# One core, three fused stages: turnings moved ahead, scores on array quarters, and weights split in small parts

## The reference

```python
hid = silu(xm @ W_h + b_h)                      # xm: patch of 16 samples and 16 ones
h = hid @ W_o + b_o + xm @ W_r + b_r
h = h + identity_attention(layernorm(h))        # corr = centred @ centred.T, softmax, @ x
y = layernorm(h)
for l in range(2):
    q, k, v = split(shift_token(y) @ wqkv[l])
    q, k = rotary(l2norm(q) * q_scale, l2norm(k) * k_scale)
    y = y + local_attention(q, k, v) @ wo[l]    # causal inside a window of 128 tokens
    a, g = split((layernorm(shift_token(y)) * lg + lb) @ w1 + b1)
    y = y + (a * gelu(g)) @ w2 + b2
out = h + y
```

## Time and profile before

| | us |
|---|---|
| median of 3 runs | 2766.34 (2763.4 to 2767.32) |
| the profiled execution | 2766.27 |
| its span, first to last instruction | 2764.5 |
| TensorE busy | 2641.3, 96% |
| DVE busy | 1918.9, 69% |
| ACT busy | 1719.4, 62% |
| POOL busy | 1399.9, 51% |
| mean granted TensorE clock | 0.984 of full speed |

### The profile page before, as it was taken

One profiled execution on the slowest core, in us unless ns is written; L12 is line 12 of the kernel. 1 busy time (PEld: TensorE's weight loads), 2 busy tenths in 40 slices (PEclk: granted clock), 3 DMA queues, 4 the chain that ended last, 5 costly groups with the idle time before them and its releaser, 6 DMA issues.

```text
span 2764.5 us, 67543 instructions
## 1 busy us (share of the span) xinstructions
PE 2641.3 (96%) x23040; PEld 2257.0 (82%) x23040; DVE 1918.9 (69%) x3771; ACT 1719.4 (62%) x4181; POOL 1399.9 (51%) x1466
## 2 busy tenths in 40 slices
PE   6999999858999999997999998999999999999998
PEld 4888888747888888886888886788888887788887
DVE  5777777547777777776655555777777777666664
ACT  3666666536777778775444444778777777444442
POOL 7888888658666666663100005866666666000000
PEclk9999999979999999999999999999999999999999
DMA  1111111111111111112211111111111111122221
GB/s 31 32 38 35 36 35 35 53 56 48 40 40 39 37 38 40 39 34 77 65 56 50 57 48 39 49 37 40 40 37 37 40 40 52 60 80 79 79 72 46
DMA packets 165603, 130.23 MB, mean 47 GB/s; under 512 B 23239, under 2 KB 163689, under 8 KB 165462
## 3 DMA queue, kind: packets, MB, share of 16 engines
q1 hardware_dynamic: 163157, 119.80, 14.0%
q0 software_dynamic: 2304, 8.47, 1.0%
HBM read 77.47 MB, written 50.33 MB: 46 GB/s over the span
## 4 chain that ended last, share of the span: by engine, by line
PE 70%; POOL 2%; SPq 2%; DVE 2%; issue 1%; DMA 1%; ACT 0%; POOLq 0%; DVEq 0%
PE const_banks L1291 6%; PE const_banks L1292 6%; PE const_banks L1293 6%; PE const_banks L1302 6%; PE const_banks L1304 6%; PE const_banks L1303 6%; PE const_banks L1389 5%; PE const_banks L1371 4%; PE const_banks L1399 4%; PE const_banks L1357 4%; PE const_banks L1418 3%; PE const_banks L1419 3%; PE const_banks L1420 3%; PE const_banks L1346 2%; PE const_banks L1344 2%; PE const_banks L1345 2%
## 5 line engine op out<-in xcount | busy, mean ns | idle before, releaser
L1019 ACT ACTIVATE attn_E<-const_banks,attn_nbias,attn_rn 128x128 f32<-128x128 f32 x1024 | 454.9, 485 | 8.6 <-DVE attn_nbias L1185 8.5
L958 POOL TENSOR_TENSOR attn_rn<-attn_ssm,const_neg_half 128x8 f32<-128x8 f32 x128 | 211.1, 1650 | 413.8 <-DVE attn_ssm L1201 313.6
L939 POOL TENSOR_TENSOR ffn_rstd<-ffn_var,const_neg_half 128x4 f32<-128x4 f32 x32 | 32.3, 1010 | 678.5 <-DVE ffn_var L1118 678.5
L952 POOL TENSOR_TENSOR attn_qk<-attn_rot_a,attn_rot_b 128x1024 f32<-128x1024 f32 x128 | 305.8, 2389 | 66.2 <-issue 55.6
L1180 DVE TENSOR_REDUCE attn_neg_top<-const_banks 128x8 f32<-128x1024 f32 x128 | 156.8, 1225 | 233.9 <-PE const_banks L1389 233.9
L1302 PE MATMUL const_banks<-weights_w_hi,attn_xT_hi 128*128 128x512 f32 x768 | 315.9, 411 | 2.6 <-ACT attn_sq L1059 2.4
L1304 PE MATMUL const_banks<-weights_w_hi,attn_xT_lo 128*128 128x512 f32 x768 | 304.6, 397 | 0.0
L1303 PE MATMUL const_banks<-weights_w_lo,attn_xT_hi 128*128 128x512 f32 x768 | 303.4, 395 | 0.0
L1217 DVE SCALAR_TENSOR_TENSOR ffn_gated<-const_banks,weights_b_col,ffn_gate 128x512 f32<-128x512 f32 (+1 forms) x192 | 143.7, 748 | 215.0 <-ACT ffn_gate L1086 207.8
L1291 PE MATMUL const_banks<-ffn_xT_hi,ffn_w_hi 128*128 128x512 f32 x704 | 282.4, 401 | 6.9 <-DVE ffn_xT_lo L1130 5.4
L1293 PE MATMUL const_banks<-ffn_xT_hi,ffn_w_lo 128*128 128x512 f32 x704 | 279.3, 397 | 0.0
(11 more groups left out here) (171 smaller groups left out, 7929.6 us busy)
## 6 DMA issues: line engine op xcount, KB each, us to landing
attn_x_res<-xa SPq DMA_DIRECT2D x128, 128.0 KB, 4.7
xb<-attn_x_new SPq DMA_DIRECT2D x128, 128.0 KB, 1.7
ffn_x_<-xb SPq DMA_DIRECT2D x32, 512.0 KB
h<-ident_h SPq DMA_DIRECT2D x64, 128.0 KB, 1.7
xa<-ident_n SPq DMA_DIRECT2D x64, 128.0 KB, 1.7
attn_x_<-xa SPq DMA_DIRECT2D x128, 64.0 KB
xa<-ffn_x_new SPq DMA_DIRECT2D x16, 512.0 KB, 3.4
ffn_add<-h SPq DMA_DIRECT2D x16, 512.0 KB, 6.9
```

The costliest lines, as they stand in the source:

```text
L952: pool.tensor_tensor(qk[:, slot].rearrange("p a n -> p (a n)"), rot_a[:].rearrange("p a h d -> p (a h d)"), rot_b[:].rearrange("p a h d -> ...
L958: pool.tensor_tensor(rn[:, slot, HEADS:], ssm[:, HEADS:], c["neg_half"][:, HEADS:], ALU.pow).then_inc(s["rn_done"], 1)
L1019: last = act.activation(E[:, r, i], ps_s[:, r, i * P:(i + 1) * P], ACT.Exp, bias=nbias[:, r, i:i + 1], scale=rn[:, slot, h:h + 1], accum_o ...
```

## The change

In the first stage: TURN stands behind SCORE in the step and no longer behind WEIGH, so that WEIGH of one step, SCORE and TURN of the next, and CENT follow each other; DONE and STORE come one step earlier; `idle` is gone; layer 0's attention weights are loaded in the steps 12, 27 and 42 and split in parts of 128 columns, one a step; POOL's list is written out. In the layers' attention: q and k, and then E, are turned before the weighting; the scores use the quarters of the array, and leave out the masked one; on ACT the high half of the output comes last; on DVE the division of E stands between the two rotary products, and the sums of squares stand ahead of the maximum; two one-element activations (`ask`) call for the tables of Exp and Gelu ahead of their first use.

```diff
-    OUT, STAT, CENT, SCORE, WEIGH, TURN, DONE, STORE = 8, 9, 10, 11, 12, 13, 14, 15
+    OUT, STAT, CENT, SCORE, WEIGH, TURN, DONE, STORE = 8, 9, 10, 11, 12, 13, 13, 14
...
-                    pool.tensor_tensor(idle[:], zero[:], zero[:], ALU.add)
                     pool.tensor_copy(hid_hi[:, slot, k], hid[:, half]).then_inc(hi_done, 1)
...
-                    if isinstance(t, int) and t in (ROWS + 5, ROWS + 7, ROWS + 9):
-                        piece = (t - ROWS - 5) // 2
-                        weights.load_attention(pool, 0, piece)
-                        weights.split_attention(pool, 0, piece)
-                run_eights(pool, ROWS, STORE, body)
+                    weights.attention_part(pool, t)
+                run_eights(pool, ROWS, STORE, body, loop=False)
...
+    def attention_part(self, pool, t):
+        for piece, first, parts in ((0, 14, 12), (1, 29, 12), (KD, 44, KI * D // P)):
+            if t == first - 2:
+                need(pool, self.a_low, self.parts)
+                self.load_attention(pool, 0, piece)
+            if first <= t < first + parts:
+                if t == first:
+                    pool.wait_ge(self.loaded, 16 * self.loads)
...
+                cols = slice((t - first) * P, (t - first + 1) * P)
+                pool.tensor_copy(hi[:, cols], self.stage[:, cols]).then_inc(self.a_high, 1)
+                self.parts += 1
+                pool.wait_ge(self.a_high, self.parts)
+                pool.tensor_tensor(lo[:, cols], self.stage[:, cols], hi[:, cols].bitcast(F32), ALU.subtract
+                                   ).then_inc(self.a_low, 1)
...
# ACT, attention of a layer
+                if step == 0 and layer:
+                    act.activation(ask[:], c["neg_half"][:, 0:1], ACT.Exp)
...
+                if step == ROWS + 4:
+                    act.activation(ask[:], c["neg_half"][:, 0:1], ACT.Gelu)
...
# TensorE, attention of a layer: the block of lag 3, which stood last, now follows the output products
+                if on(3):
+                    b = t - 3
+                    need(pe, s["et_done"], 2 * b)
+                    for r, dst in ((0, ps_q), (1, ps_k)):
+                        need(pe, s["kT_done" if r else "qT_done"], min_int(b + 2, L + ROWS))
+                        need(pe, s["en_done"], 2 * b + r + 1)
+                        for j in range(HEADS // 2):
+                            last = pe.transpose(dst[:, j * P:(j + 1) * P], E[:, r, j], c["ident"][:])
+                        last.then_inc(s["e_ps"], 1)
...
-                    need(pe, s["qT_done"], b + 1)
-                    need(pe, s["kT_done"], b + 1)
                     for j in range(HEADS // 2):
                         for r in range(2):
                             part = slice(r * HD, (r + 1) * HD)
-                            last = pe.matmul(ps_s[:, r, j * P:(j + 1) * P], qT[part, j], kT[part, j], start=False,
-                                             stop=True, skip_group_check=True)
+                            pe.matmul(ps_s[0:HD, r, j * P:j * P + HD], qT[part, j, 0:HD], kT[part, j, 0:HD],
+                                      start=False, stop=True, skip_group_check=True)
+                            last = pe.matmul(ps_s[HD:P, r, j * P:(j + 1) * P], qT[part, j, HD:P], kT[part, j],
+                                             start=False, stop=True, skip_group_check=True)
                     last.then_inc(s["s_ps"], 1)
```

96 lines of the change are left out of this document (50 added, 46 removed).

## The result

The changed kernel takes 2724.5 us (median; 2724.05 to 2724.97 in 4 runs) against 2764.9 for the kernel before (2763.0 to 2767.3 in 4 runs): a ratio of 0.9853, 95% interval 0.9836 to 0.9871. It is faster by 40 us; 52 were forecast, and 2724.5 lies in the range. Whether the 40 us came from the terms of the sum is another matter. The profiled execution of the changed kernel has a span of 2723.2 us.

The account below looks back on a forecast made before the run. The tensor engine was taken to bind, so its list had to get shorter. Attention 25, first stage 11, drain 12 and small terms 4 sum to 52 us off 2766.3: 2714 us, range 2700 to 2728.

Parts of the forecast that it names:

- The scores: Attention: scores in the rule's quarters save 0.12 + 0.10 us a row, 0.21 taken; no gain from the masked quarter.
- Does anything else then bind?: Attention: the loop through DVE takes 9.91 us, 0.08 under the tensor engine's 9.99, so it was taken as hidden.
- rival 1: Attention: the DVE loop binds, or the scores' change is still paid; about 10.2 us a row, 2739 us; chance 0.25.
- Rivals 3 and 4: Scores: quarters sharing rows run serially (3: about 2769 us, chance 0.05) or also await each other's weights (4: 2955, 0.04).
- Rival 2: Scores: masked quarter counts, 0.2 us more a row, but the loop stops it after 0.08; 2704 us; chance 0.06.
- The turning of E: Attention: turning E before the weighting adds no matmul and is reached with 0.7 us to spare.
- The turning of q and k: Attention: turning them earlier adds no matmul; waits in a layer's first steps taken as zero, 8 us either side.
- First stage: First stage: two changes of the array's parts instead of three, 55 rows x 0.2 = 11 us (0 to 16).
- Drain: End of the first stage: waits behind split weights go and the pipe is a step shorter; 12 us (7 to 18).
- Small terms: Attention ends: earlier squares of the last two rows and earlier Gelu table loads, 4 us in all (0 to 7).

Follow-up runs that it names:

- run 3: The changed kernel with the scores on halves of the rows again (16 matmuls instead of 32): 2741.8 us, ratio 0.9912.
- run 9: The changed kernel with E turned behind the scores again, all else as in the change: 2725.7 us, ratio 0.9855.
- run 6: Kernel before plus first-stage change and score quarters, q and k turned ahead of the output products; DVE and ACT in old order: 2865.0 us, ratio 1.0360.
- run 7: The changed kernel with only the squares' sum back behind the maximum: 3139.7 us, ratio 1.1367.
- run 2: The kernel before with only TURN moved behind SCORE and the write-back a step earlier: 2753.1 us, ratio 0.9949.
- run 1: The kernel before with only the first-stage part of the change, attention left old: 2741.5 us, ratio 0.9906.
- run 8: The changed kernel with the second rotary product ahead of the division of E again: 3119.0 us, ratio 1.1249.
- run 10: The changed kernel with the second rotary product done for q then k, each half squared once rotated: 2712.8 us, ratio 0.9811.
- run 11: The kernel of run 9 with the second rotary product done for q then k, each half squared once rotated: 2716.2 us, ratio 0.9817.

## Why the prediction was right, and where not

**Right in the outcome:** faster, 40 us for 52, inside the range.

**The scores: mechanism right, size too small.** Both pieces of the forecast showed. Behind the rule's 512 columns the first score comes at 0.24 us instead of 0.34, and the first pair's 0.1 is gone: between the first two pairs on halves lay 0.21 us (run 3) where all others had 0.11, and on quarters it is 0.11 there too. That is about the 0.21 taken. The other 0.1 is the masked quarter, at which I took no gain: the 128-column scores stand behind the rule's 256 columns and start at 0.14 already, while the 64-column ones have room. With 128 columns in every quarter the last score would start at 0.24 + 7 x 0.11 = 1.01 instead of 0.91, an estimate from these starts; no run had such quarters. The change of the array's parts behind the scores stayed, as said.

**The step that failed: "Does anything else then bind?"** The chain was named term by term, and the terms that are instructions sum to 9.69 us for the 9.71 forecast (the sums and ssm together 1.35, from start to start). Mis-sized were the handings over: four at 0.05, taken from one row in which DVE had followed TensorE, are 0.31 together. rot_b's end to the squares is 0.12 (911.99 to 912.11), the squares' end to their sums 0.13 (913.13 to 913.26). With them the chain is 10.00 us, and 10.08 where the bias is handed over in 0.28. The forecast's 0.08 us of margin was smaller than this error, and since the tensor engine became faster than thought, the chain was not 0.08 under its time but 0.12 to 0.20 over it. The extra 0.1 of the scores brought nothing: the chain alone allows 10.00 to 10.08. That is rival 1, with a smaller loss than it was given. The forty middle rows gave 0.12 to 0.16 instead of 0.21, by which 120 rows are 14 to 19 us for the 25 forecast; the run with the old attention puts the whole of the attention at 17. So the total lies in the range with one term a third too large, and not because each term held.

**Rivals 3 and 4: wrong.** The quarters of one half of the rows run at once and do not wait for each other's weights: the 128-column records start 0.11 us apart with quarters that share their rows. A load of a 64-column quarter's weights starts at 903.36 and takes 0.13 us, while matmuls on both halves of the rows run from 903.26 to 903.53. The rule of the Trainium skill ("TensorE: Matmul & The Clock Gate", Part 3), by which a load overlaps only when the row group differs, would have made this change slower by the forecast's 215 us. This trace contradicts it, as WEIGH's strips did in the earlier trace rows. **Rival 2: half right.** The masked quarter counts, by some 0.1 us of the 0.2 that it was given, and the loop kept that from the time.

**The turning of E:** no cost, shown by run 9. **The turning of q and k:** costs nothing only because the squares are summed earlier; without that the kernel is slower than before by 99 us (run 6, whose counterpart is run 9: 139 us between them) or by 373 (run 7, the fall of the clock included). The forecast saw POOL's q and k as a matter of the first steps of a layer (0 with 8 on either side). There the first ten periods of layer 0 sum to 99.4 us for 104.4 before (96.1 for 97.5 in layer 1); but run 2, with the old attention, has 99.1 too, and run 1 101.8. So nothing speaks against the zero, and no gain is shown.

**First stage: right.** The rows gain 11 us (443.4 to 432.3 in run 2), 11 forecast; WEIGH to the end of CENT takes 3.46 us, 3.5 forecast. **Drain: right.** 83.0 - 69.7 = 13 us in the changed kernel's profile and 9.5 in run 1's, 12 forecast; of these the shorter pipe alone is 2.5 (run 2), some 3 forecast. By the medians both together are 24 us (run 1), 23 forecast.

**Small terms: not seen.** 4 us of gain were forecast in the stretches behind the last rows; in the two profiles these are 0.7 and 3.2 us longer. The run with only the first stage changed has 449 us in the last stretch too, so the 3.2 do not show a loss by the attention's change. On a term this small the runs give no verdict.

## What to carry to other kernels

When a chain of other engines is worked out to less than 1% under the binding engine's time, treat it as binding: count each handing over at what such a pair of engines shows (here 0.12 us from rot_b to the squares and 0.13 back), and test it by shortening the chain, not the engine. Before an operation is moved earlier, follow its input back through the slow engine to the place in the queue that feeds it: of the four pieces of the change that were undone one by one (runs 3, 7, 8 and 9) two left the kernel slower than it was before. When such a wait opens, read the granted clock as well: it took 1.5 us a step more in run 8. Put matmuls of like array parts next to each other; here a change of parts cost 0.1 to 0.2 us. Neither the busy share of the tensor engine nor the shares of the chain that ended last tells which engine binds; the times from step to step do.

## What the hardware showed that was not expected

- The scores start 0.14 us behind the rule when both are quarters, and 0.34 when the scores use halves, and the first pair's 0.1 goes too: 0.32 us in all for one group. The two halves of the array's columns keep their own pace: 128-column scores behind 256 columns of the rule start 0.11 us apart, 64-column ones behind 512 start 0.06 us apart.
- A DVE operation with two operands from SBUF that starts beside POOL's addition, which reads SBUF, takes 2.64 us for 0.69. In runs 10 and 11 ssm shows it too (0.55 to 0.65 us for 0.18), on the chain that sets the step of run 11. The Trainium skill ("SBUF — State Buffer", "SBUF: two separate sides") calls the pair of ports that both use an exclusive lock for the whole instruction, taken by whoever starts first; the trace agrees in both directions, since DVE's second operation ended 0.55 us behind POOL's, and POOL's, which started 0.02 us behind DVE's first, took 2.89 us for 2.37.
- Behind a wait in the middle of the weighting the matmuls started 0.14 us after the copy of kT had ended: the weighting was 0.22 us longer, where the same wait ahead of the scores had cost nothing.
- The granted clock fell in steps in which the tensor engine had stood idle for about 2 us waiting for E or for q and k: steps of runs 7 and 8 that take 11.8 to 12.6 us at full clock take 13.5 to 14.2 with over 3 us at 1.2 GHz. In the middle rows of run 6, with some 1 us of idle time in each step, it stayed at 1.00.
- In two of four steps ACT starts the exponentials 0.28 instead of 0.20 us behind the bias. Why was not found.
